# Seven of 128 row loads issued as 126 rows and 2 rows, in a cross-network kernel

## The reference

```python
def step(x, wb):
    wi, bi = wb
    xw = jnp.matmul(x, wi)          # one number for each row
    x_new = x0 * xw + bi + x
```

## Time and profile before

| | us |
|---|---|
| median of 3 runs | 1281.98 (1280.91 to 1282.07) |
| profiled execution | 1280.2 |
| its span, first to last instruction | 1278.4 |
| granted TensorE clock, mean | 0.782 |

### The profile page before, as it was taken

One profiled execution on the slowest core, in us unless ns is written; L12 is line 12 of the kernel. 1 busy time (PEld: TensorE's weight loads), 2 busy tenths in 40 slices (PEclk: granted clock), 3 DMA queues, 4 the chain that ended last, 5 costly groups with the idle time before them and its releaser, 6 DMA issues.

```text
span 1278.4 us, 20057 instructions
## 1 busy us (share of the span) xinstructions
PE 780.7 (61%) x9114; PEld 728.6 (57%) x9114; DVE 1150.2 (90%) x526; ACT 102.7 (8%) x345; POOL 4.3 (0%) x17
## 2 busy tenths in 40 slices
PE   8666666555656655556555665665655665665653
PEld 4666566555556655555545565565655654665653
DVE  5999999898988988989889898898998988989896
ACT  3000000000000000000000000000000000000010
POOL 1000000000000000000000000000000000000000
PEclk9877787887877778778787777777777778678677
DMA  9999999999999999999999999999999999999996
GB/s 385 416 380 428 430 431 431 429 427 429 433 429 431 431 430 432 430 431 424 421 424 425 418 427 421 424 425 422 427 424 421 424 423 425 425 423 425 426 421 286
DMA packets 37385, 537.28 MB, mean 420 GB/s; under 512 B 4168, under 2 KB 4168, under 8 KB 4728
## 3 DMA queue, kind: packets, MB, share of 16 engines
q1 hardware_dynamic: 18432, 268.44, 50.1%
q10 hardware_dynamic: 18936, 268.64, 49.3%
HBM read 268.63 MB, written 268.44 MB: 420 GB/s over the span
## 4 chain that ended last, share of the span: by engine, by line
DMA 72%; DVE 15%; PE 8%; issue 3%; ACT 1%; DVEq 0%
DMA out_dram<-tiles 56%; DMA tiles<-in_r_inputs_dram 15%; DVE tiles L286 8%; DVE blocks L264 7%; PE dots L401 6%; ACT spread L197 1%; PE dots L359 1%; PE scratch L339 1%; DMA tiles<-in_L_rec_w_dram 0%; PE strips L334 0%; PE strips L349 0%; ACT c_last L189 0%; PE turned L370 0%; DVE scale L275 0%; DVEq L42 0%
## 5 line engine op out<-in xcount | busy, mean ns | idle before, releaser
L401 PE MATMUL dots<-blocks,weights 128*64 128x128 f32 x7808 | 662.6, 349 | 380.8 <-DVE blocks L264 380.6
L401 PEld LDWEIGHTS dots<-blocks,weights 128*64 128x64 f32 x7808 | 628.7, 185 | 405.3 <-DVE blocks L264 405.2
L264 DVE STREAM_TRANSPOSE blocks<-tiles 128x2048 f32<-128x2048 f32 x256 | 576.0, 2288 | 100.1 <-issue 100.1
L286 DVE SCALAR_TENSOR_TENSOR tiles<-tiles,scale,c_last 128x4096 f32<-128x4096 f32 (+1 forms) x131 | 571.9, 4368 | 0.2
L197 ACT ACTIVATE spread<-dots,group_mask 128x128 f32<-128x128 f32 (+1 forms) x268 | 75.2, 363 | 1062.6 <-PE dots L401 1020.3
L370 PE MATMUL turned<-layer_sel,spread 128*128 128x8 f32 x512 | 68.1, 258 | 85.5 <-ACT spread L197 85.5
L370 PEld LDWEIGHTS turned<-layer_sel,spread 128*128 128x128 f32 x512 | 62.3, 191 | 101.4 <-issue 95.6
L359 PE MATMUL dots<-blocks,weights 128*64 128x64 f32 x768 | 32.4, 266 | 11.0 <-DVE blocks L264 11.0
L359 PEld LDWEIGHTS dots<-blocks,weights 128*64 128x64 f32 x768 | 31.7, 180 | 12.9 <-issue 12.9
L205 ACT ACTIVATE growth<-turned,ones 128x16 f32<-128x16 f32 (+1 forms) x67 | 18.3, 273 | 85.0 <-PE turned L370 85.0
L275 DVE TENSOR_TENSOR_SCAN scale<-growth,cw 128x6 f32<-128x6 f32 x128 | 13.3, 142 | 8.9 <-ACT growth L205 8.9
(11 more groups left out here) (25 smaller groups left out, 11.3 us busy)
## 6 DMA issues: line engine op xcount, KB each, us to landing
tiles<-in_r_inputs_dram SPq DMA_DIRECT2D x128, 2048.0 KB, 14.9
out_dram<-tiles ACTq DMA_DIRECT2D x127, 2048.0 KB, 25.5
out_dram<-tiles ACTq DMA_DIRECT2D x4, 512.0 KB, 7.0
tiles<-in_L_rec_w_dram ACTq DMA_DIRECT2D x1, 96.0 KB
tiles<-in_L_rec_b_dram ACTq DMA_DIRECT2D x1, 96.0 KB
```

Source lines behind the costliest of these rows:

```text
L264: nc.vector.transpose(blocks[:, p % PLACES, :], source).then_inc(blocks_ready, 1)
L286: nc.vector.scalar_tensor_tensor(out=tiles[:, s, at], in0=tiles[:, s, at], scalar=scale[:, u % 2, t, L - 1:L], in1=c_last[:, at], op0=ALU. ...
L401: last = nc.tensor.matmul(dots[at:at + KM * Q, :, :, :], weights[:, c * CH // Q + k:c * CH // Q + k + KM, :], place[:, :, k * Q:(k + KM) * Q],
```

## The change

Loads 10, 28, 46, 64, 82, 100 and 118 (n % 18 == 10) are issued as two transfers, one of the tile's first 126 rows and one of its last 2 rows, on the same queue and one right behind the other. Both raise the same semaphore by 16, so it gets 32 for such a load; `landed_by(n)` adds up what a slot's semaphore has to show when tile n has landed, and DVE waits for that. The bytes, the slots, the order of loads and all other work are as before.

```diff
+MOST = 126
+EVERY, FIRST = 18, 10
...
+        def in_two(n):
+            return n % EVERY == FIRST
+
+        def landed_by(n):
+            return sum(32 if in_two(m) else 16 for m in range(n % N_SLOTS, n + 1, N_SLOTS))
...
                 sp.wait_ge(y_stored[s], n // N_SLOTS * 16)
-                sp.dma_start(tiles[:, s, :], x[n * P:(n + 1) * P, :]).then_inc(x_landed[s], 16)
+                if in_two(n):
+                    sp.dma_start(tiles[0:MOST, s, :], x[n * P:n * P + MOST, :]).then_inc(x_landed[s], 16)
+                    sp.dma_start(tiles[MOST:P, s, :], x[n * P + MOST:(n + 1) * P, :]).then_inc(x_landed[s], 16)
+                else:
+                    sp.dma_start(tiles[:, s, :], x[n * P:(n + 1) * P, :]).then_inc(x_landed[s], 16)
...
-                    dve.wait_ge(x_landed[n % N_SLOTS], (n // N_SLOTS + 1) * 16)
+                    dve.wait_ge(x_landed[n % N_SLOTS], landed_by(n))
```

## The result

The changed kernel takes 1299.91 us (median of 4 runs, 1299.83 to 1302.19), the kernel before 1281.45 us beside it: a ratio of 1.0148, 95% interval 1.0131 to 1.0166. That is slower by 19.0 us (16.8 to 21.3), 2.7 us for each of the seven split loads. The prediction had the sign, but 1286 us and a range to 1291 us. The profiled run took 1299.85 us with a span of 1298.0 us, against 1280.2 and 1278.4 us.

What follows compares the result with a forecast made beforehand. The prediction took one slow DMA engine, at 0.619 us a row, to bound the kernel. Its extra rows added about 4.0 us to 1282.0 us, other terms nothing: 1286 us, range 1271 to 1291, own range 1284 to 1289.

Steps and rivals of the forecast that it cites:

- The spare of 0.15 us a tile: Time per tile that engines other than the slow one have to spare, 2.7 us between two splits.
- point 1: Split loads: 126 rows run on 14 engines, 9 each; 2 rows on 2 engines, one each; two engines get nothing.
- point 2: Slow engine gets one more row in each of seven split loads, 0.619 us each: +3.7 to +4.3 us.
- points 3 and 6: Second issue on SP, 0.328 us seven times, which nothing waits for; counts of 32 for DVE's waits: nothing.
- point 5: Nine rows on one engine in a split load: extra from nothing to 5.5 us per load, lower end taken.
- the nine rows get in each other's way: Rival: in split loads two engines write the same part of SBUF; +20 us, 1302 us, up to 1320; chance 0.05.
- The rate after 650 us: Sign in the changed profile: 430 and not 424 GB/s if the slow engine was relieved.
- The longest landing: Sign for rows in each other's way: longest load landing far above 16.1 us, median unchanged.
- tail of a single engine: Sign: in the last microseconds a single engine works if the forecast is right; none if the slow engine was relieved.
- The slow engine left out: Rival: split loads give the slow engine 56 rows less; faster, 1269 to 1274, centre 1272 us; chance 0.20.
- hit twice: Rival: slow engine also gets a row of each 2-row transfer, 14 rows, +8.7 us, 1290.6 us; chance 0.07.
- No change: Rival: extra rows fall where the slow engine's work is put off anyway; 1282 us, up to 1284; chance 0.12.

Runs made afterwards that it cites:

- the probes: Kernel before plus sixteen transfers of 1 to 16 rows of 8 bytes, each behind one store with its own semaphore; 1281.5 us.
- The column halves: Kernel before with the same seven loads as two transfers of 128 rows and half the columns each; ratio 1.0028, +3.6 us.

## Why the prediction was wrong

**What bounds the kernel: right.** The DMA engines do, and one of them is slow; the probes found a single late one, the fifth. Misread was the step from 430 to 424 GB/s: I had the other engines fall idle a little, but the share stays 1.01 in the earlier trace rows, and a row of the loads takes longer instead: by the share and the bytes of queue 1, 0.613 us from 240 to 500 us and 0.633 us from 650 to 1200. The spare of 0.15 us a tile, on which a rival rests, is thus not seen as idle time.

The Trainium skill (DMA: Bandwidth & Descriptors, Latency and other measured facts) says that engines 7 and 15 are usually the slower ones; if its numbers follow the order in which transfers take engines, no run here agrees, and the measurement decides.

**Engines per load, point 1: right.** The packet counts are unchanged at 18,432 and 18,936, as 14 and 2 closing packets demand, and a probe of k rows, k up to 16, has k landings.

**The term of the slow engine, point 2: right in sign, about right in size, but not the main term.** 0.619 us a row was used; the 20 extra rows from SBUF cost 0.70 us each (0.42 to 0.98), the seven from memory to memory 0.97 (0.62 to 1.3). That explains some 4 to 7 of the 19.0 us. The even split 112 and 16 loses 23 us without it.

**The second issue and the counts, points 3 and 6: nothing speaks against them.** Leaving the second transfer out brought nothing back. The column halves cost 3.6 us, which may be an upper bound for two transfers a tile.

**The spread over SBUF, point 5: the step that failed.** I bounded nine rows' extra time from 0 to 5.5 us a load and took the lower end, because the 24-row loads had not held the other engines up. Those loads are 48 rows of a quarter of the length against 128 long ones, so the earlier trace rows could hardly show a halved rate; its right reading was that it says nothing. The trace of before even has a hint the other way. From 6 to 8 us, while the second 24-row load is moved, its view of queue 1 reads

```profile
q1 hardware_dynamic: 43, 0.70, 98.9%
```

or 0.74 us for each of 43 long rows in place of 0.61; what slowed them no run shows. Alone, the split tile takes 10.7 us in place of 4.9 (12.3 as 112 and 16), +5.8 us, and the tile behind it lands 7.8 us late, so even my upper end was too low. In the whole kernel the seven splits cost 2.7 us each on average.

How the one becomes the other is open. At split 100 the dip in the rate is worth 1.1 us and not 5.5, a part of the loss stands between the splits, and the lasting loss may be in it. The rival "the nine rows get in each other's way" had the mechanism, 2.8 us a load, and 1302 us; it had 0.05 of the chances, and the range left it out. Its reason for paying half was wrong all the same: I let a spare of 2.7 us between two splits absorb the rest. With fourteen splits that spare is half as large, (5.5 - 1.35) x 14 = 58 us would have been lost, and 32 us were. That its 1302 us is so near to the measured 1299.9 is luck. Nor does it need nine rows: eight do as well.

**The signs to look for.** The rate after 650 us fell to 415 GB/s; I had looked for 424 or 430. The longest landing rose to 23.1 us from 16.1, as the rival asked, but the median rose as well, 14.9 to 19.6 us. That sign was a poor one: with 14 rows from memory to memory, where no tile is divided, the median is 22.2 us. And the end has no tail of a single engine; from 1295.6 to 1297 us the changed kernel shows all of them at work,

```profile
q10 hardware_dynamic: 153, 0.56, 100.9%
```

where the earlier trace rows had one. One engine is still late in the steady part (in load 99 one landing comes 8.6 us after the last but one, where it was 0.9), but the others have lost their lead in stores by the end.

**The other rivals.** The slow engine left out, or hit twice: neither, as in the probe run it is the fifth. No change: no.

## What to carry to other kernels

The same 2 MB took 4.9 us or 9.5 to 12.3 us here by the form of the transfer alone: before a tile of 128 partitions is divided by partitions to move work between engines, time the form alone, in a stretch without other traffic. When a bound has far ends and the rows nearest to it could not have shown the bad end, the bad end is not unlikely, and belongs into the range. A slow engine is best found by probes: small transfers of 1 to 16 rows, each with its own semaphore, in the middle of the traffic.

## What the runs showed of the hardware that I had not expected

- A 2 MB tile moved to SBUF alone, by two transfers that divide its 128 partitions, ran at 205 to 231 GB/s against 426 whole (115 GB/s while a part of 16 rows was moved), whether the engines' rows were even (112 and 16, 64 and 64) or not (126 and 2); memory to memory the same forms differed by under 1 us in 6.
- In the run with probes the late engine was the fifth in the order in which transfers take engines, 15 to 18 us behind the first one there after a store; the slow engine of the kernel before is some 1.5% slower than the others (0.619 against 0.610 us a row).
- A loss of about 10 us that lasts to the end of the kernel came in 4 of 10 runs with one split load, at 416 GB/s in place of 424 in the profiled one, and in 1 of 25 runs without any. Why is open.
